# Target and source passes of a graph kernel: bias and one product change engines, edge weights copied earlier

## The chip, the cores and the metric

The kernel runs on one core of one Trainium2 chip. The metric is the device time of one execution in microseconds. Before the change it is 4458.62 us, the median of three runs (4454.08 to 4461.81).

## What is computed

Four graph layers over 100000 nodes of 128 features, 25000 edges sorted by target. Every layer ends in `x = layernorm(x + layer(x))`.

```python
# layer 0: attributes of the edges summed at their target, a small network, residual
agg = segment_sum(e_flat, dst)                      # 160 wide
h = (softplus(agg @ W1.T + b1) - log 2) @ W2.T + b2
x = layernorm(x + (x + h))
# layer 1: weighted neighbours, divided by max(sum of edge weights, 1)
# layer 2: relu(x @ w_s + segment_sum((x @ w_n)[src], dst))
# layer 3: relu(cheb(x, W1, b1)) (256 wide), then cheb(h, W2, b2), three terms each
```

Most nodes are the target of no edge. For them every layer depends on the node's own row alone. Only nodes that are a target get sums from edges.

## The kernel before

An edge pass or a row pass works on quads: 4 tiles of 128 rows, 512 rows in a turn. 25000 edges make 49 quads (`QUADS`), the nodes 196 blocks. The passes run one after the other, with a seam (`enter`, `leave`) at which all five engines wait for each other:

- `tgt0` (the target pass): layer 0 at the targets of the edges, 49 turns, about 310 to 666 us
- `src0` (the source pass): for the sources of the edges, all layers as if no edge came in, stored as state 1, 2, 3 and the hidden state h, 49 turns, about 666 to 1177 us
- `nodes`: the same for all nodes, 196 turns, up to about 2580 us
- `L1`, `L2`, `T1`, `T2`, `LH`, `LU`: the layers with their edge sums, 49 turns each

Every engine runs its own list of instructions in order, written out by hand for turn g, with stages of older quads (`g.less(k)`, in the code g1 to g5) in the same turn. Semaphores (`signal`, `transfer`) order the engines. `s.wait(engine, pass, g, back=k)` waits until the signal of turn g - k is given. Most tiles have two buffers (`g.b`), `rows` has four (`g.r`, `RING`).

**Target pass.** SP loads 512 rows of edge attributes into `rows` three turns ahead (L437). POOL copies the edge weights beside them as column 160 (`put_weights`, L551) and gathers the targets' rows of x by four indirect DMAs (`gather`, L540), which wait for DVE's L880 of two turns before, since `xin` has two buffers. In a turn POOL gathers first and copies for turn g + 2 behind that. PE's turn (L1402) is: transposes for quad g + 1 (L1316, L1318; they wait for `attr_in` and `ew_put`), first product of quad g (L1329, L1330), the sums of weights turned into a column by 1x1 products (L1334), second product of quad g - 1 (L1387). DVE's turn is L849, two scans (L810), L864, then for quad g - 2 L877, L880, the moments (L818, L822), and the marks for the next quad (L791). ACT computes the softplus of quad g - 1, the norm of g - 3 and the root of g - 2.

**Source pass.** POOL's turn: y0 of quad g + 1 (L575), gathers for g + 3 (L540). DVE's turn: statistics of y0 (L926, L931), L959, L962, L969, four L976 (y1), four L982 (x1), L990 (u2), its statistics, L1011, L1014, L1018 (reciprocal `rs1`), and four L1022: the second state x2 of quad g - 1 into `x3b`, a row scaled by `rs1`. ACT's turn: copies of the transposed y0 and y1, L1211 (relu of the 256-wide h of quad g - 4, from PSUM into `hb`), two roots (L1081), the copy yTc, the squares (L1223), x3 (L1234). PE's turn: three groups of transposes (L1298), L1441, L1447, and last h of quad g - 3: for each of four tiles L1466 (one row of ones times the bias row, 256 wide) and L1467 added onto it; before these it waits for `h_kept` of the turn before. SP stores x1, x2, x3 and h in this order (L472).

## Time and profile before

| | |
|---|---|
| median of 3 runs | 4458.62 us |
| the profiled execution | 4466.06 us, of which its span is 4464.0 us |
| PE busy | 3560.5 us (80%) |
| DVE busy | 3173.4 us (71%) |
| ACT busy | 2444.6 us (55%) |
| POOL busy | 3007.1 us (67%) |
| mean granted TensorE clock | 0.889 |

The page gives averages over passes with different limits. A pass is therefore read by a view of its own stretch: the busy time in it, the waits in it, and one turn in order of time. "Idle before" in square brackets is how long the engine stood before an instruction, and what ended that; "issue" is an end that the profile doesn't see. Instructions of one line that follow each other are merged ("x4"). "PEld" (weight loads) is left out below. PE shows a float32 product as two passes.

### The profile page before, as it was taken

The page shows a single profiled execution, that of the slowest core. Times are in us where ns is not written, and L with a number is a line of the kernel's source. Part 1 is how long each engine was busy: PE and PEld are TensorE (multiplying, and loading weights), DVE is VectorE, ACT ScalarE, POOL GpSimd, SP SyncE. Part 2 cuts the span into 40 slices and gives each one's busy share as a digit, 9 for nine tenths or more (in the row PEclk, how much of TensorE's full clock was granted, in tenths as well). Part 3 has the DMA queues.
Part 4 walks back from the last instruction along what each step waited for, and adds up shares of the span by engine and source line. Part 5 has one row for each costly group of instructions (what it writes and reads, how often), then busy time and mean ns, then how long its engine had stood idle before and what let it go on. Part 6 is the DMA issues. An engine that isn't in the chain of part 4 may idle for free. (4 is left out here: it accounts for less than half of the span.)

```text
span 4464.0 us, 77093 instructions
## 1 busy us (share of the span) xinstructions
PE 3560.5 (80%) x21778; PEld 2728.0 (61%) x21778; DVE 3173.4 (71%) x13414; ACT 2444.6 (55%) x7163; POOL 3007.1 (67%) x3450
## 2 busy tenths in 40 slices
PE   6868887999899999999999956566898989931111
PEld 3336655766588888888888746565455768831111
DVE  8988876677588888888888868788222446655555
ACT  0006665666588888888888856311565764421111
POOL 0006656555388888888888767576775757767777
PEclk9989997888899999999999978888999999965555
DMA  0015643444222222222222235454676987843332
GB/s 19 1 45 155 166 133 127 164 166 167 100 77 77 77 76 77 76 76 76 77 77 77 68 123 156 127 157 143 221 247 217 310 288 247 260 140 93 98 94 77
DMA packets 307439, 575.11 MB, mean 129 GB/s; under 512 B 65310, under 2 KB 93783, under 8 KB 307018
## 3 DMA queue, kind: packets, MB, share of 16 engines
q1 hardware_dynamic: 234890, 442.75, 29.4%
q0 software_dynamic: 72128, 127.43, 10.9%
q8 instruction: 180, 2.95, 0.3%
q14 instruction: 241, 1.97, 0.1%
HBM read 300.83 MB, written 270.68 MB: 128 GB/s over the span
## 5 line engine op out<-in xcount | busy, mean ns | idle before, releaser
L1316 PE MATMUL ps<-ident,rows 128*128 128x128 f32 x1372 | 280.9, 310 | 605.2 <-ACT rows L1093 498.3
L540 POOL DMA_INDIRECT rows<-state,rows_of_src x588 | 557.4, 948 | 252.6 <-issue 171.7
L1093 ACT ACTIVATE rows<-rows,lap_w 128x128 f32<-128x128 f32 (+1 forms) x784 | 270.7, 419 | 607.3 <-DMA rows<-lap,rows_of_lap 480.0
L1316 PEld LDWEIGHTS ps<-ident,rows 128*128 128x128 f32 x1372 | 191.4, 159 | 672.7 <-ACT rows L1093 453.6
L810 DVE TENSOR_TENSOR_SCAN x<-same,x,ps 128x512 f32<-128x512 uint8 x336 | 429.0, 1277 | 236.5 <-PE ps L1316 204.6
L1076 ACT ACTIVATE yTa<-ps 128x512 f32<-128x512 f32 x392 | 233.5, 596 | 607.8 <-PE ps L1298 607.6
L540 POOL DMA_INDIRECT rows<-lap,rows_of_lap x392 | 390.5, 996 | 168.5 <-issue 117.1
L618 POOL DMA_INDIRECT lk<-node_table,look_idx x392 | 384.6, 981 | 92.1 <-issue 83.6
L575 POOL TENSOR_TENSOR y<-xin,c0h 128x512 f32<-128x512 f32 x245 | 310.8, 1269 | 200.0 <-DVE outb L982 142.6
L926 DVE BATCH_NORM_STATS2 bn<-y 128x6 f32<-128x128 f32 x1764 | 378.6, 276 | 42.8 <-POOL y L575 42.7
L1454 PE MATMUL ps<-V,hT 128*128 128x128 f32 x3136 | 402.0, 281 | 5.5 <-ACT hT L1206 5.5
L593 POOL TENSOR_SCALAR x<-u,negm,rs 128x128 f32<-128x128 f32 x784 | 342.2, 446 | 74.6 <-DVE rs L959 74.0
L1454 PEld LDWEIGHTS ps<-V,hT 128*128 128x128 f32 x3136 | 364.8, 191 | 43.1 <-ACT hT L1206 43.1
L1461 PE MATMUL ps<-yTc,G 128*128 128x512 f32 x784 | 369.0, 593 | 1.9 <-ACT yTc L1076 1.9
L1298 PEld LDWEIGHTS ps<-ident,y 128*128 128x128 f32 x1960 | 251.3, 151 | 149.6 <-issue 133.9
L1241 ACT ACTIVATE outb<-y,off,rs 128x128 f32<-128x128 f32 x784 | 322.6, 491 | 0.4 <-DVE off L954 0.4
L1298 PE MATMUL ps<-ident,y 128*128 128x128 f32 x1960 | 280.5, 290 | 36.5 <-POOL y L575 33.5
L1223 ACT ACTIVATE unused<-y 128x128 bf16<-128x128 f32 x980 | 290.3, 313 | 0.0
L1441 PE MATMUL ps<-A,yTa 128*128 128x128 f32 x1960 | 288.6, 292 | 1.8 <-ACT yTa L1076 1.7
L540 POOL DMA_INDIRECT xin<-in_x_dram,dst_g x196 | 197.4, 1007 | 136.1 <-DVE y L880 90.7
L976 DVE SCALAR_TENSOR_TENSOR y<-ps,rs,b1c 128x128 f32<-128x128 f32 x980 | 276.2, 345 | 17.2 <-PE ps L1441 6.7
L1081 ACT ACTIVATE sd<-mv,consts 128x4 f32<-128x4 f32 x588 | 174.2, 296 | 192.1 <-DVE mv L822 139.4
(253 smaller groups left out, 9601.1 us busy)
## 6 DMA issues: line engine op xcount, KB each, us to landing
state_h<-hb SPq DMA_DIRECT2D x98, 512.0 KB, 3.9
xin<-in_x_dram SPq DMA_DIRECT2D x196, 256.0 KB, 2.8
out_dram<-outb SPq DMA_DIRECT2D x196, 256.0 KB, 2.1
xe<-state SPq DMA_DIRECT2D x147, 256.0 KB
state<-outb SPq DMA_DIRECT2D x98, 256.0 KB, 2.1
state<-oe SPq DMA_DIRECT2D x98, 256.0 KB, 2.1
h_pre<-hb SPq DMA_DIRECT2D x49, 512.0 KB, 3.1
rows<-in_edge_attr_10x_dram SPq DMA_DIRECT2D x48, 320.0 KB, 3.2
```

The lines of the kernel that those rows point to most:

```text
L540: gp.indirect_dma_start(out=dest[:, at, k, 0:width], out_offset=None, in_=table_, in_offset=bass.IndirectOffsetOnAxis(ap=index[:, c:c + 1] ...
L575: gp.tensor_tensor(y0[:, g.b], xin[:, g.b], all4(c0h[:, :]), ALU.add).then_inc(y0_made.sem, 1)
L593: i = gp.tensor_scalar(x3[:, g2.b, k, :], u2[:, g2.b, k, :], negm[:, g2.b, k:k + 1], rs[:, 2, g2.b, k:k + 1], ALU.add, ALU.mult)
L618: gp.indirect_dma_start(out=lk[:, g.b, 2 * j:2 * j + 2], out_offset=None, in_=node_table, in_offset=bass.IndirectOffsetOnAxis(ap=look_idx[ ...
L810: v.tensor_tensor_scan(t[0:np_, g.b].rearrange("p k d -> p (k d)"), same[0:np_, 512 * g.c:512 * g.c + 512], ps[0:np_, bk + g.b, :], t[0:np ...
L926: i = v.bn_stats(bn[:, n, k, :], y[:, k, :])
L1223: i = a.activation(unused[:, k, :], y1[:, g1.b, k, :], ACT.Square, accum_out=ssum[:, g1.b, k:k + 1])
L1241: i = a.activation(outb[:, g5.b, k, :], y3[:, g5.b, k, :], ACT.Identity, bias=off3[:, g5.b, k:k + 1], scale=rs[:, 3, g5.b, k:k + 1])
L1298: i = t.transpose(bank(bk)[:, k, :], source[:, k, :], ident[:, :])
L1316: i = t.transpose(bank(g.b)[:, k, :], rows[:, g.r, k, 0:P], ident[:, :])
L1454: i = t.matmul(bank(7)[:, k, :], hT[:, j, k, :], V02[:, j, :], start=j == 0, stop=j == 1)
L1461: i = t.matmul(ps[:, 5 + j, :], G02[:, j * P:(j + 1) * P], yTc[:].rearrange("p k d -> p (k d)"), start=True, stop=True)
```

## The change

In the target pass `put_weights` moves in front of the turn's gathers and to turn g + 3, with three copies ahead of the loop, and the four 1x1 products of L1334 become transposes.

In the source pass PE no longer adds the bias: its products start at L1467. DVE adds it, at the end of its turn, from PSUM into `hb` (signal `h_biased`). ACT's relu then runs on `hb` in place, behind x3. The second state is shared: DVE makes tiles 0 to 2 (signal `x2_most`) and POOL tile 3 (signal `x2_made`), in POOL's turn behind the gathers; SP waits for both, and DVE's next write of y1 in that buffer waits for POOL's. PE's last step waits for `h_biased` instead of `h_kept`.

```diff
--- before.py
+++ after.py
@@ -239,7 +239,8 @@
         u2_made, bn2, mv2, tv2, rs2 = (signal(n, "src0 nodes") for n in ("u2_made", "bn2", "mv2", "tv2", "rs2"))
         y3_made, bn3, mv3, rs3, off3_made, looked_up = (
             signal(n, "nodes") for n in ("y3_made", "bn3", "mv3", "rs3", "off3_made", "looked_up"))
-        x1_made, rs1, x2_made, off2 = (signal(n, "src0") for n in ("x1_made", "rs1", "x2_made", "off2"))
+        x1_made, rs1, x2_made, x2_most, h_biased, off2 = (
+            signal(n, "src0") for n in ("x1_made", "rs1", "x2_made", "x2_most", "h_biased", "off2"))
 
         same_made, ew_put, ws_turned, ws_taken, ws_max = (
             signal(n, "tgt0") for n in ("same_made", "ew_put", "ws_turned", "ws_taken", "ws_max"))
@@ -469,6 +470,8 @@
                                                 (x3_made, g.less(2), state3, x3, x3_st), (h_kept, g.less(4), state_h, hb, h_st)):
                     if g_.inside(QUADS):
                         signal_.wait(sp, "src0", g_)
+                        if signal_ is x2_made:
+                            x2_most.wait(sp, "src0", g_)
                         sp.dma_start(quad_of(t, g_, 1), buf[:, g_.b]).then_inc(tr.of(g_), 16)
 
             enter(sp, "src0")
@@ -556,11 +559,11 @@
                     last = g.less(-3)
                     summed.wait(pool, "tgt0", last, back=RING)
                     gp.memset(rows[:, last.r, 3, 0:ATTR], 0.0).then_inc(zeroed, 1)
+                put_weights(g.less(-3))
                 gather("tgt0", g, x, dst_g, xin, g.b, P, x_gathered, [(step, 2)])
-                put_weights(g.less(-2))
-
-            put_weights(Turn(0))
-            put_weights(Turn(1))
+
+            for c in range(3):
+                put_weights(Turn(c))
 
             run_turns(QUADS, 0, tgt0_turn)
             leave(pool)
@@ -576,7 +579,7 @@
 
             def row_pass(p, n, meanwhile):
                 def turn(g):
-                    next_, g2, g3 = g.less(-1), g.less(2), g.less(3)
+                    next_, g1, g2, g3 = g.less(-1), g.less(1), g.less(2), g.less(3)
                     if next_.inside(n):
                         make_y0(p, next_)
                     if p == "nodes" and g3.inside(n):
@@ -584,6 +587,11 @@
                         y3_made.wait(pool, p, g3, back=2)
                         gp.tensor_tensor(x3b[:, g3.b], x3[:, g3.b], all4(gb2_row[:, :]), ALU.add).then_inc(x3b_made.sem, 1)
                     meanwhile(g)
+                    if p == "src0" and g1.inside(n):
+                        rs1.wait(pool, p, g1)
+                        more_st.wait(pool, p, g1, back=2)
+                        gp.tensor_scalar(x3b[:, g1.b, 3, :], y1[:, g1.b, 3, :], rs[:, 1, g1.b, 3:4], None, ALU.mult)\
+                            .then_inc(x2_made.sem, 1)
                     if p == "nodes" and g2.inside(n):
 
                         x3_turned.wait(pool, p, g2, back=2)
@@ -972,6 +980,8 @@
                         p1_made.wait(dve, p, g)
                         y1_turned.wait(dve, p, g, back=2)
                         squared.wait(dve, p, g, back=2)
+                        if not nodes:
+                            x2_made.wait(dve, p, g, back=2)
                         for k in range(4):
                             i = v.scalar_tensor_tensor(y1[:, g.b, k, :], bank(3)[:, k, :], dev(0, g.b, k), b1c[:, :],
                                                        ALU.mult, ALU.add)
@@ -1018,9 +1028,13 @@
                             v.reciprocal(rs[:, 1, g1.b, :], sd[:, 1, g1.b, :]).then_inc(rs1.sem, 1)
                             rs1.wait(dve, p, g1)
                             more_st.wait(dve, p, g1, back=2)
-                            for k in range(4):
+                            for k in range(3):
                                 i = v.tensor_scalar(x3b[:, g1.b, k, :], y1[:, g1.b, k, :], dev(1, g1.b, k), None, ALU.mult)
-                            i.then_inc(x2_made.sem, 1)
+                            i.then_inc(x2_most.sem, 1)
+                    if i3 and not nodes:
+                        h_made.wait(dve, p, g3)
+                        h_st.wait(dve, p, g3, back=2)
+                        v.tensor_tensor(hb[:, g3.b], wide(5), all4(gb1_row[:, :]), ALU.add).then_inc(h_biased.sem, 1)
 
                 enter(dve, p)
                 run_turns(n, 5, turn)
@@ -1205,10 +1219,6 @@
                         for j in range(2):
                             a.activation(hT[:, j], bank(5 + j), ACT.Relu, bias=gb1_col[:, j:j + 1])\
                                 .then_inc(hidden.sem, 1)
-                    if g4.inside(n) and not nodes:
-                        h_made.wait(act, p, g4)
-                        h_st.wait(act, p, g4, back=2)
-                        a.activation(hb[:, g4.b], wide(5), ACT.Relu).then_inc(h_kept.sem, 1)
                     if g2.inside(n):
                         root(p, g2, sd2, tv2, sd[:, 2, g2.b, :], tmpv[:, g2.b, :], EPS2)
                     if g.inside(n):
@@ -1234,6 +1244,9 @@
                             i = a.activation(x3[:, g2.b, k, :], u2[:, g2.b, k, :], ACT.Identity, bias=off3[:, g2.b, k:k + 1],
                                              scale=rs[:, 2, g2.b, k:k + 1])
                         i.then_inc(x3_made.sem, 1)
+                    if g4.inside(n) and not nodes:
+                        h_biased.wait(act, p, g4)
+                        a.activation(hb[:, g4.b], hb[:, g4.b], ACT.Relu).then_inc(h_kept.sem, 1)
                     if nodes and g5.inside(n):
                         off3_made.wait(act, p, g5)
                         out_st.wait(act, p, g5, back=2)
@@ -1331,7 +1344,7 @@
                                  start=False, stop=True).then_inc(first_product.sem, 1)
                         ws_taken.wait(pe, p, g, back=1)
                         for k in range(4):
-                            i = t.matmul(ps[:, 4, k:k + 1], agg_b[32:33, g.b, k, :], ones[32:33, 0:1], start=True, stop=True)
+                            i = t.transpose(ps[:, 4, k:k + 1], agg_b[32:33, g.b, k, :], ident[32:33, 32:33])
                         i.then_inc(ws_turned.sem, 1)
                     if p == "L1":
                         own, near = SELF[g.b], NEIGH[g.b]
@@ -1461,10 +1474,9 @@
                                 i = t.matmul(ps[:, 5 + j, :], G02[:, j * P:(j + 1) * P], yTc[:].rearrange("p k d -> p (k d)"),
                                              start=True, stop=True)
                         else:
-                            h_kept.wait(pe, p, g3, back=1)
+                            h_biased.wait(pe, p, g3, back=1)
                             for k in range(4):
-                                t.matmul(wide(5)[:, k, :], ones[0:1, :], gb1_row[0:1, :], start=True, stop=False)
-                                i = t.matmul(wide(5)[:, k, :], yTc[:, k, :], G02[:, :], start=False, stop=True)
+                                i = t.matmul(wide(5)[:, k, :], yTc[:, k, :], G02[:, :], start=True, stop=True)
                         i.then_inc(h_made.sem, 1)
 
                 enter(pe, p)
```

## Rows read from the trace of the kernel before

**Rows 1.** Stretches: busy us by engine in five columns, granted clock, DMA share, GB/s.

```profile
330.00:650.00 320.00, 281.38 (x1685) 201.49 (x1684) 271.20 (x743) 209.16 (x464) 194.75 (x230) 0.99 0.56 156
...
720.00:1140.00 420.00, 415.75 (x1956) 292.32 (x1955) 301.02 (x1552) 263.04 (x851) 213.50 (x207) 0.87 0.46 164
...
2620.00:2900.00 280.00, 181.18 (x1234) 168.92 (x1232) 224.13 (x767) 151.53 (x459) 189.61 (x201) 0.85 0.47 144
```

**Rows 2.** Waits, 330 to 650 us: total, times, longest.

```profile
POOL xin L540 <- DVE y L880: 88.8, 46, 16.5
```

**Rows 3.** Timeline of one target turn: start us, duration us, engine, line.

```profile
500.06 0.30 PE L1316 MATMUL ps<-ident,rows 128*128 128x128 f32 x1 [0.56 <-issue]
...
500.88 0.69 DVE L880 TENSOR_TENSOR y<-y,xin 128x512 f32<-128x512 f32 x1
...
501.85 0.97 POOL L540 DMA_INDIRECT xin<-in_x_dram,dst_g  x1 [1.89 <-DVE y L880]
...
502.81 0.66 DVE L791 TENSOR_TENSOR same<-dst_in 128x512 uint8<-128x512 int32 x1
...
504.05 0.16 DVE L849 TENSOR_SCALAR tmpv<-ps 128x4 f32<-128x4 f32 x1 [0.58 <-PE ps L1334]
...
506.79 0.21 POOL L551 COPY rows<-ew_col 128x4 f32<-128x4 f32 x1
...
507.09 0.30 PE L1316 MATMUL ps<-ident,rows 128*128 128x128 f32 x1 [1.10 <-issue]
...
507.38 0.69 DVE L880 TENSOR_TENSOR y<-y,xin 128x512 f32<-128x512 f32 x1
```

**Rows 4.** Timeline, DVE: L877 in turns 0 and 46 of the target pass.

```profile
337.66 0.69 DVE L877 SCALAR_TENSOR_TENSOR y<-ps,b2h 128x512 f32<-128x512 f32 x1 [0.99 <-PE ps L1387]
...
649.22 0.65 DVE L877 SCALAR_TENSOR_TENSOR y<-ps,b2h 128x512 f32<-128x512 f32 x1
```

**Rows 5.** Timeline of one source turn, around PE's last step.

```profile
902.41 0.18 DVE L959 RECIPROCAL rs<-sd 128x4 f32<-128x4 f32 x1 [2.80 <-ACT sd L1081]
...
903.11 0.69 PE L1466 MATMUL ps<-gb_row,ones 1*128 1x256 f32 x2
...
907.37 0.88 DVE L1022 TENSOR_SCALAR x3b<-y,rs 128x128 f32<-128x128 f32 x4
...
908.16 0.87 DVE L926 BATCH_NORM_STATS2 bn<-y 128x6 f32<-128x128 f32 x4
...
908.24 1.91 PE L1298 MATMUL ps<-ident,y 128*128 128x128 f32 x8
...
909.06 0.38 DVE L931 BATCH_NORM_AGGREGATE mv<-bn 128x2 f32<-128x6 f32 x4
```

**Rows 6.** Timeline, DVE: L976 in turns 4 and 48 of the source pass.

```profile
720.95 1.13 DVE L976 SCALAR_TENSOR_TENSOR y<-ps,rs,b1c 128x128 f32<-128x128 f32 x4
...
1137.92 1.13 DVE L976 SCALAR_TENSOR_TENSOR y<-ps,rs,b1c 128x128 f32<-128x128 f32 x4
```

**Rows 7.** Opening of the source pass (timeline), and L1022's durations in ns (min/median/max).

```profile
703.26 2.38 DVE L1022 TENSOR_SCALAR x3b<-y,rs 128x128 f32<-128x128 f32 x4
...
703.65 1.27 POOL L575 TENSOR_TENSOR y<-xin,c0h 128x512 f32<-128x512 f32 x1
...
L1022 DVE TENSOR_SCALAR x3b<-y,rs x196: 273/282/1755, 695.5 to 1148.9; 128x128 f32<-128x128 f32 x196
```

**Rows 8.** Durations of nearest operations (ns min/median/max; last row: busy, mean ns).

```profile
L996 DVE TENSOR_TENSOR y<-ps,x3b x196: 679/681/692, 1207.4 to 2570.6; 128x512 f32<-128x512 f32 x196
...
L860 DVE TENSOR_TENSOR hT<-ps,y x25: 1224/1225/1225, 3419.0 to 3662.6; 128x1024 f32<-128x1024 f32 x25
...
L593 POOL TENSOR_SCALAR x<-u,negm,rs x784: 441/444/459, 1193.0 to 2559.1; 128x128 f32<-128x128 f32 x196
...
L1081 ACT ACTIVATE sd<-mv,consts 128x4 f32<-128x4 f32 x588 | 174.2, 296 | 192.1 <-DVE mv L822 139.4
```

**Rows 9.** Timeline, PE: a 256-wide pair at the end of the source pass.

```profile
1155.86 1.22 PE L1467 MATMUL ps<-G,yTc 128*128 128x256 f32 x2
```


## What I expect

> **What bounds the kernel now.** I read the busy time by stretch first [rows 1]. The change touches two passes. In the target pass (330 to 650 us) no engine is full: PE is busy 281 of 320 us, DVE 271, POOL 195. In the source pass (720 to 1140 us) PE is full, 416 of 420 us. So the first is held by a loop of waits, the second by PE's own work.
>
> Target pass: the waits say who stands still [rows 2]. POOL waits 88.8 us for DVE's L880 in 46 turns. A wait alone is no cause, so I follow one turn in time [rows 3]. L880 ends at 501.57 (500.88 + 0.69); POOL's first gather starts at 501.85; four gathers and then the copy of the edge weights (L551) at 506.79, over at 507.0; PE's transposes restart at 507.09. The reader should see that PE starts within 0.1 us of the copy's end although the profile calls the wait "issue": the copy is the last of PE's inputs. From there PE needs 500.06 to 504.05 = 3.99 us to give DVE its weight column, and DVE needs 504.05 to 507.38, plus 0.69, = 4.02 us to the end of the next L880. The loop spans two turns: 0.28 + 5.24 (501.85 to 507.09) + 3.99 + 4.02 = 13.53, or 6.77 us a turn. The measured one is (649.22 - 337.66)/46 = 6.773 us [rows 4]. They agree, so the loop is the bound.
>
> Source pass: in one turn PE runs its last step, eight pairs of 256-wide matmuls, from 903.11 to 908.24 = 5.13 us, and goes straight into the next turn [rows 5]. DVE stands 2.80 us before L959, because ACT's relu (L1211) waits behind PE and stands before the root that L959 needs. The turn is (1137.92 - 720.95)/44 = 9.48 us [rows 6].
>
> **Target pass, the change.** The copy moves before the gathers and one turn further ahead. It waits for the transposes four turns before the row that it fills, which PE finished over a turn earlier, so it runs while POOL stands before its gathers (1.9 us a turn, 88.8/46 [rows 2]) and leaves the loop. Behind it in POOL's queue are only the gathers of the same turn. The four one-column products become transposes, one pass of four instead of two; PE was not the bound, so that is costed at nothing as long as DVE is late. What is late next is DVE's own chain: 504.05 to 507.38 = 3.33, then 500.88 to 502.81 = 1.93, then L791's 0.66 = 5.92 us [rows 3]. PE has 281/(320/6.77) = 5.95 us of work [rows 1] before the four passes leave; it fits, barely. POOL has 5.24 us. So 6.77 becomes 5.92: 0.85 a turn, 46 turns, 39 us. One doubt: the copy (about 0.2 us) now falls at L880, which reads two SBUF tiles; if they exclude each other it costs up to 0.2 us x 46 = 9 us, or nothing if the copy yields. I take 36 us, range 28 to 41.
>
> **Source pass, what leaves.** Four of eight pairs on PE: half of 5.13, so PE's turn falls to about 6.9 us at today's mean clock. ACT's relu moves behind the work that DVE waits for, so the 2.80 us goes. PE is no longer the bound; DVE is next. Its chain from starts [rows 5]: L959 to L1022 902.41 to 907.37 = 4.96; L1022's four products 0.79 (to 908.16); L926 to L931 0.90; L931 to L959 about 0.3 (four aggregates, 0.38 long, overlapped). Sum 6.95.
>
> **Source pass, what comes.** One product leaves DVE: -0.20. The bias comes, one 128x1024 addition from PSUM plus SBUF; the T2 pass has that shape at 1.22 us (L860) and it overlaps its neighbour a little [rows 8]: +1.2. With the relu gone DVE still waits for one short ACT root between L931 and L969: the root takes 0.296 us [rows 8], and L959 and L962 run meanwhile; I estimate +0.14, between 0 and 0.3. That is 8.09 us without interference. ACT has 263/(420/9.48) = 5.9 us of work a turn [rows 1] and PE 6.9, both below. The product on POOL costs 0.444 us there [rows 8]; POOL's turn is 0.28 (its reaction to L880, [rows 3]) + 0.44 + 1.27 (L575, [rows 7]) + 4.94 (four gathers, 501.85 to 506.79) and another 0.28 = 7.2 us, below 8.1. But it is in front of the next L575 and, through that, the next gathers: both slip from behind L982 to behind L1018. L575's result is first used by L926 a whole turn after the one at 908.16; the slip, L982 to L1018, is well under half a turn and is covered. SP's store of the second state waits a little longer, and three stores queue behind it; hb has two buffers, so its store has about a turn to land: no cost. PE waits for DVE's bias of the turn before instead of ACT's relu: it is done before PE comes to that step.
>
> **The unknown cost is DVE against POOL.** When the pass starts, L1022 began at 703.26 and four products took 2.38 us instead of 0.87, while POOL's L575 ran from 703.65 to 704.92 [rows 7]. The longest product took 1755 ns against a median of 282, so it ended (705.01) just after POOL's instruction had. So a SBUF-to-SBUF product of DVE stands still during a POOL instruction on SBUF. L996, from PSUM, ran 196 times beside busy POOL in 679 to 692 ns [rows 8]; the new bias is of that kind and safe. The new POOL product, however, is released by the very reciprocal that releases DVE's three products, and L575 follows it at once. Bounds: nothing, if DVE gets its three in first; +0.25 a turn, if POOL's product stops one of them and DVE gets in before L575; +1.5, if DVE stands until L575 is over (0.28 + 0.44 + 1.27 + 0.1 = 2.1 us after the reciprocal, against 0.7 unhindered, and one or two products after that). I take +0.25: 8.35 us a turn, nearest to the row in which exactly one instruction of POOL was sat out.
>
> The Trainium skill, SBUF — State Buffer, section Who interferes with whom, says that VectorE and GpSimd share one port pair as an exclusive lock, that the one that issues first keeps it for its whole instruction, and that the other fully blocks. By that rule, the trace agrees: the one long L1022 took 1755 ns against 282. The rule speaks against this change, since both products are released together; by it alone the block would last 0.44 us, near my value, if the lock is free between two POOL instructions.
>
> Sum: 44 turns x (9.48 - 8.35) = 50 us. At both ends of the pass the pairs run at the low clock level, 1.22 us each [rows 9]: one step of four fewer at the start, two at the end, 4.9 us each, less the bias and relu that now follow the last one and what other engines hold back: 11 us. Source pass 61, target pass 36, together 97. The profiled execution took 4466.1 us (span 4464.0), so 4369; it lies 7.4 above the median 4458.6, so **4362 us**.
>
> **Rivals.** (a) DVE first, no block: 8.09 a turn, 44 x 1.39 + 11 + 36 = 108, **4351 us**. For it: DVE reacts faster than POOL. Chance 0.17. (b) The lock passes straight from POOL's product to L575: 9.6 a turn, 44 x (-0.12) + 11 + 36 = 42, **4417 us**. For it: POOL's instructions stand in its queue with satisfied waits, and in [rows 7] POOL kept DVE out before its own record began. Against: no row shows DVE skipped twice. Chance 0.27. (c) The copy was not alone last in the target pass, some other input of PE arrives with it and the turn stays near 6.7: 61 only, **4398 us**. Against: the loop adds up to 6.77 with it. Chance 0.07. (d) In the source pass something of the chain ACT, PE, DVE holds the turn near 8.9: 25 + 11 + 36 = 72, **4387 us**. Chance 0.06. (e) Slower: the clock. PE's granted clock was 0.87 in the source pass although PE was full, 0.99 in the target pass at 88% busy, and 0.85 in the L1 pass at 65% [rows 1]. PE falls to some 70% busy. If it stayed at the low level (1.2 GHz) all through, PE's turn would be (9.48 - 5.13) x 0.87/0.5 = 7.6, plus 4 x 1.22 = 4.9, = 12.5 us: 44 x 3.0 = 133 lost, 36 + 11 won, **4545 us**. It binds once over a third of a turn is at the low level, and costs time overall from about three quarters. Against: the L1 pass is no busier and has 0.85. Chance 0.03.
>
> **How the numbers follow.** My forecast has 0.40. The range takes in (a) and (b) with the doubt on the copy: 4340 to 4428, leaving out (e) and tails. A measurement of this kernel tells 0.2% (9 us) from no change. Faster 0.94, same 0.03 (a poor (b) with a poor target pass), slower 0.03.
>
> **What the profile after would show.** L877's starts 5.9 us apart, POOL's copy in its idle time, PE's wait before L1316 gone or ended by DVE. In the source pass L976 8.3 apart, DVE over 90% busy, no 2.80 us wait before L959. The group of L1022's three products tells the cases apart: (a) 0.67 us, forecast about 0.9, (b) over 2. L540 and L575 must follow POOL's product. The prediction is wrong if DVE's three products and L575 overlap otherwise than said, if the turn is set by PE at a granted clock under 0.7, or if L877's period stays over 6.3.

## The result and the profile after

| | before | after |
|---|---|---|
| median of four runs | 4457.76 us | 4344.89 us (4341.65 to 4350.78) |
| the profiled execution | 4466.06 us, span 4464.0 | 4350.78 us, span 4348.7 |
| mean granted TensorE clock | 0.889 | 0.902 |

The ratio is 0.9748 [0.9731, 0.9765]: 113 us faster. The forecast was 4362, so 17 us too slow, inside its range.

Lines have moved: L877 is now L885, L880 is L888, L810 is L818, L540 is L543, L551 is L554, L575 is L578, L926 is L934, L931 is L939, L959 is L967, L976 is L986, L1018 is L1028, L1022 is L1032, L1081 is L1095, L1467 is L1479. New are POOL's product at L593 and DVE's bias at L1037.

Stretches of the changed kernel, columns as in [rows 1]: the target pass, the source pass, the L1 pass.

```profile
330.00:610.00 280.00, 253.49 (x1496) 168.42 (x1494) 268.97 (x739) 204.10 (x459) 198.87 (x227) 0.99 0.60 178
680.00:1060.00 380.00, 254.78 (x1633) 212.17 (x1631) 353.47 (x1575) 270.73 (x864) 248.52 (x254) 0.99 0.54 193
2500.00:2790.00 290.00, 184.93 (x1284) 172.18 (x1285) 235.72 (x809) 156.15 (x470) 199.27 (x212) 0.87 0.48 147
```

DVE is now the fullest engine in both passes: 269 of 280 us and 353 of 380. PE fell to 67% of the source pass, and its granted clock rose from 0.87 [rows 1] to 0.99.

The target pass: the wait of POOL and of PE, over 330 to 600 us (total, times, longest), and then DVE's L885 of turns 0 and 45 with one turn between them in order of time.

```profile
POOL xin L543 <- DVE y L888: 39.6, 42, 12.9
PE ps L1342 <- DVE x3b L818: 26.5, 44, 0.7
```

```profile
336.86 0.69 DVE L885 SCALAR_TENSOR_TENSOR y<-ps,b2h 128x512 f32<-128x512 f32 x1 [0.65 <-PE ps L1400]
...
502.36 0.27 PE L1329 MATMUL ps<-ident,rows 128*128 128x128 f32 x1
...
503.98 1.12 PE L1342 MATMUL ps<-x,W1Ta 128*128 128x512 f32 x2 [0.58 <-DVE x3b L818]
...
504.60 0.78 DVE L888 TENSOR_TENSOR y<-y,xin 128x512 f32<-128x512 f32 x1
...
505.25 0.21 POOL L554 COPY rows<-ew_col 128x4 f32<-128x4 f32 x1
...
605.32 0.65 DVE L885 SCALAR_TENSOR_TENSOR y<-ps,b2h 128x512 f32<-128x512 f32 x1
```

L888 and the copy L554 over the whole pass (ns, minimum, median, maximum):

```profile
L888 DVE TENSOR_TENSOR y<-y,xin x49: 691/718/778, 337.6 to 624.1; 128x512 f32<-128x512 f32 x49
L554 POOL COPY rows<-ew_col x49: 189/199/767, 310.5 to 594.2; 128x4 f32<-128x4 f32 x49
```

The period is (605.32 - 336.86)/45 = 5.97 us, against 6.77 [rows 4]. PE's wait before the transposes is gone. What it waits for now is DVE's scan. POOL's copy (505.25) no longer stands behind the gathers. The turn shown has the longest L888 of all, 0.78 us instead of 0.69 [rows 3]; the median is 0.72, and where no copy runs beside it L888 stays at 0.69. In about a quarter of the turns it is the copy that gets longer, up to 0.77 us instead of 0.20, and L888 stays at 0.69 to 0.70.

One source turn of the changed kernel, against [rows 5]:

```profile
860.38 0.17 DVE L1028 RECIPROCAL rs<-sd 128x4 f32<-128x4 f32 x1
860.59 0.84 DVE L1032 TENSOR_SCALAR x3b<-y,rs 128x128 f32<-128x128 f32 x3
860.65 0.69 POOL L593 TENSOR_SCALAR x3b<-y,rs 128x128 f32<-128x128 f32 x1 [1.08 <-DVE rs L1028]
...
861.30 1.21 DVE L1037 TENSOR_TENSOR hb<-ps,gb_row 128x1024 f32<-128x1024 f32 x1
861.33 1.26 POOL L578 TENSOR_TENSOR y<-xin,c0h 128x512 f32<-128x512 f32 x1
...
862.44 0.85 DVE L934 BATCH_NORM_STATS2 bn<-y 128x6 f32<-128x128 f32 x4
...
863.33 0.38 DVE L939 BATCH_NORM_AGGREGATE mv<-bn 128x2 f32<-128x6 f32 x4
863.62 0.14 DVE L967 RECIPROCAL rs<-sd 128x4 f32<-128x4 f32 x1
863.74 0.30 ACT L1095 ACTIVATE sd<-mv,consts 128x4 f32<-128x4 f32 x1 [2.25 <-DVE mv L939]
...
864.57 1.99 PE L1479 MATMUL ps<-G,yTc 128*128 128x256 f32 x8 [1.65 <-ACT yTc L1090]
```

DVE goes from one instruction to the next without a wait. ACT waits for it (2.25 us), and PE for ACT (1.65 us). The turn, from L986 of turn 4 to that of turn 48, against [rows 6]:

```profile
676.68 1.12 DVE L986 SCALAR_TENSOR_TENSOR y<-ps,rs,b1c 128x128 f32<-128x128 f32 x4
...
1035.71 1.12 DVE L986 SCALAR_TENSOR_TENSOR y<-ps,rs,b1c 128x128 f32<-128x128 f32 x4
```

That is 359.03/44 = 8.16 us instead of 9.48. The durations of the two halves of the shared product (ns, minimum, median, maximum):

```profile
L1032 DVE TENSOR_SCALAR x3b<-y,rs x147: 281/326/404, 657.6 to 1045.2; 128x128 f32<-128x128 f32 x147
L593 POOL TENSOR_SCALAR x3b<-y,rs x49: 623/695/722, 659.4 to 1044.8; 128x128 f32<-128x128 f32 x49
```

By their starts, DVE's second product follows the first after 0.20 us, as in the kernel before, and the third follows the second after 0.32 us instead of 0.20; so the bias behind them starts 0.12 us later, in nearly every turn. The durations overlap and say less. POOL's 695 ns can't be set against the 444 of [rows 8], a median over products of the node pass that follow each other four at a time: in the bias-first run below this product takes 603 ns with no product of DVE beside it, and 602 with no instruction of DVE beside it at all (1062.89 us). So POOL's loses 0.09 us.

**Where the 115 us of span went.** The source pass's first y0 starts 38.0 us earlier (640.55 against 678.51): the target pass. The node pass's first y0 starts 117.9 us earlier (1061.17 against 1179.07), so the source pass gave 79.9: 44 turns 57.9, its opening (from the first y0 to L986 of turn 4) 6.3, its end 15.7. The later passes took back 2.6.

### The profile page after: what moved, and what is told of

It reads as the page before. It is cut to its first block and busy times, and to the rows that moved or that the text cites. A ratio compares the mean times of both kernels' runs of the same rounds, so it can differ in the third digit from the quotient of the medians.

```text
span 4348.7 us, 76062 instructions
## 1 busy us (share of the span) xinstructions
PE 3337.6 (77%) x21190; PEld 2595.4 (60%) x21190; DVE 3221.5 (74%) x13414; ACT 2442.3 (56%) x7163; POOL 3051.8 (70%) x3499
## 5 line engine op out<-in xcount | busy, mean ns | idle before, releaser
L543 POOL DMA_INDIRECT rows<-state,rows_of_src x588 | 557.0, 947 | 249.2 <-issue 173.2
L818 DVE TENSOR_TENSOR_SCAN x<-same,x,ps 128x512 f32<-128x512 uint8 x336 | 428.9, 1276 | 237.5 <-PE ps L1329 204.0
L543 POOL DMA_INDIRECT rows<-lap,rows_of_lap x392 | 391.7, 999 | 167.3 <-issue 117.7
L1467 PE MATMUL ps<-V,hT 128*128 128x128 f32 x3136 | 402.7, 282 | 5.7 <-ACT hT L1220 5.7
L934 DVE BATCH_NORM_STATS2 bn<-y 128x6 f32<-128x128 f32 x1764 | 378.2, 275 | 23.4 <-POOL y L578 23.3
L1467 PEld LDWEIGHTS ps<-V,hT 128*128 128x128 f32 x3136 | 365.4, 192 | 43.2 <-ACT hT L1220 43.2
L1095 ACT ACTIVATE sd<-mv,consts 128x4 f32<-128x4 f32 x588 | 174.1, 296 | 276.5 <-DVE mv L939 152.9
L578 POOL TENSOR_TENSOR y<-xin,c0h 128x512 f32<-128x512 f32 x245 | 311.1, 1270 | 15.9 <-DMA xin<-in_x_dram 15.9
L1311 PEld LDWEIGHTS ps<-ident,y 128*128 128x128 f32 x1960 | 232.8, 143 | 146.2 <-issue 130.6
L1311 PE MATMUL ps<-ident,y 128*128 128x128 f32 x1960 | 259.9, 276 | 37.1 <-POOL y L578 34.7
L986 DVE SCALAR_TENSOR_TENSOR y<-ps,rs,b1c 128x128 f32<-128x128 f32 x980 | 276.2, 344 | 14.0 <-PE ps L1454 3.9
L1454 PEld LDWEIGHTS ps<-A,yTa 128*128 128x128 f32 x1960 | 242.1, 194 | 56.7 <-ACT yTa L1090 46.7
```

The costliest lines, as they stand in the source:

```text
L543: gp.indirect_dma_start(out=dest[:, at, k, 0:width], out_offset=None, in_=table_, in_offset=bass.IndirectOffsetOnAxis(ap=index[:, c:c + 1] ...
L578: gp.tensor_tensor(y0[:, g.b], xin[:, g.b], all4(c0h[:, :]), ALU.add).then_inc(y0_made.sem, 1)
L818: v.tensor_tensor_scan(t[0:np_, g.b].rearrange("p k d -> p (k d)"), same[0:np_, 512 * g.c:512 * g.c + 512], ps[0:np_, bk + g.b, :], t[0:np ...
L934: i = v.bn_stats(bn[:, n, k, :], y[:, k, :])
L1311: i = t.transpose(bank(bk)[:, k, :], source[:, k, :], ident[:, :])
L1454: i = t.matmul(bank(3)[:, k, :], yTa[:, k, :], A1[:, :], start=True, stop=True)
```

## The experiments

My theory: in the target pass the copy is the last link of the loop; in the source pass DVE sets the turn, and POOL's product costs it little because it doesn't fall beside POOL's long instruction. The rivals: PE's fewer passes, not the copy, shorten the target turn; POOL's product is worth nothing or harms; the relu's new place did it; and PE lost its time not to the amount of bias work but to how that work was cut. Runs of one group shared a chip with runs of the kernel before. A source turn is the mean over 44 turns, read as above.

### First group: the two halves, and the two edits of the target pass

The kernel before took 4460.24 us here.

**The target edits alone**: the changed kernel, with the source pass of before.

```diff
-                            h_biased.wait(pe, p, g3, back=1)
+                            h_kept.wait(pe, p, g3, back=1)
                             for k in range(4):
-                                i = t.matmul(wide(5)[:, k, :], yTc[:, k, :], G02[:, :], start=True, stop=True)
+                                t.matmul(wide(5)[:, k, :], ones[0:1, :], gb1_row[0:1, :], start=True, stop=False)
+                                i = t.matmul(wide(5)[:, k, :], yTc[:, k, :], G02[:, :], start=False, stop=True)
```

> The kernel before with the target pass's two edits alone. My theory: the two passes are independent, so this keeps the whole target gain, about 38 us (period of L877's line 6.77 to 5.97 us), and the source pass stays at 9.48 us a turn: about 4420 us, ratio 0.9915. Rival: part of the later passes' gain comes from shifted phases, then the two single-pass kernels don't add up to the 113 us of both.

Measured: 4417.7 us, ratio 0.9902 [0.9882, 0.9921], 42.5 us less. The target turn is 5.97, the source turn stays near 9.5.

**The source edits alone**: the changed kernel, with the target pass of before.

```diff
-                put_weights(g.less(-3))
                 gather("tgt0", g, x, dst_g, xin, g.b, P, x_gathered, [(step, 2)])
+                put_weights(g.less(-2))
...
-                            i = t.transpose(ps[:, 4, k:k + 1], agg_b[32:33, g.b, k, :], ident[32:33, 32:33])
+                            i = t.matmul(ps[:, 4, k:k + 1], agg_b[32:33, g.b, k, :], ones[32:33, 0:1], start=True, stop=True)
```

> The kernel before with the source pass's edits alone. My theory: the source pass gains 80 us, of which 58 in 44 steady turns (9.48 to 8.16 us) and 22 at its opening and its end; the target pass stays at 6.77 us: about 4378 us, ratio 0.982. Rival as for the target edits: the sum of both differs from 113 us by over 5.

Measured: 4386.0 us, 0.9833 [0.9816, 0.9851], 74.2 less. The source turn is 8.17, the target turn alternates 6.45 and 7.08, mean 6.77. The halves add up to 116.7 against 113 for both, inside the intervals: no sign that the two parts share a bound.

**The copy alone**: the kernel before, the copy moved, the 1x1 products kept.

```diff
+                put_weights(g.less(-3))
                 gather("tgt0", g, x, dst_g, xin, g.b, P, x_gathered, [(step, 2)])
-                put_weights(g.less(-2))
```

> The kernel before with only the copy of the edge weights moved; the four one-column products stay products. Theory A (the copy was the last link of a two-turn loop, 13.5 us): the period falls to about 6.0 us, set by PE's 5.95 us of work and DVE's 5.9; gain 35 us or more of the 38. Rival B (the shorter weight column on PE was the gain): the period stays above 6.5 us, gain under 12 us.

Measured: 4421.95 us, 0.9916 [0.9898, 0.9934], 38.3 less. Its timeline, two following L877:

```profile
500.50 0.65 DVE L877 SCALAR_TENSOR_TENSOR y<-ps,b2h 128x512 f32<-128x512 f32 x1
...
506.46 0.65 DVE L877 SCALAR_TENSOR_TENSOR y<-ps,b2h 128x512 f32<-128x512 f32 x1
```

5.96 us, and 6.01 as the mean over 46 turns: the copy alone gives nearly the whole gain in the turn. It was the last link of the loop.

**The transposes alone**: the kernel before, the 1x1 products turned into transposes, the copy left behind the gathers.

```diff
-                            i = t.matmul(ps[:, 4, k:k + 1], agg_b[32:33, g.b, k, :], ones[32:33, 0:1], start=True, stop=True)
+                            i = t.transpose(ps[:, 4, k:k + 1], agg_b[32:33, g.b, k, :], ident[32:33, 32:33])
```

> The kernel before with only the four one-column products made transposes. Theory A: the loop of two turns gets shorter by the passes that leave, some 0.5 to 0.6 us, so the period falls from 6.77 to about 6.5: gain 12 us. Rival B: period about 6.0 us, gain 35 us or more.

Measured: 4439.26 us, 0.995 [0.9934, 0.9966], 21.0 less where some 12 were expected. Its timeline:

```profile
490.50 0.65 DVE L877 SCALAR_TENSOR_TENSOR y<-ps,b2h 128x512 f32<-128x512 f32 x1
497.29 0.65 DVE L877 SCALAR_TENSOR_TENSOR y<-ps,b2h 128x512 f32<-128x512 f32 x1
...
503.89 0.20 POOL L551 COPY rows<-ew_col 128x4 f32<-128x4 f32 x1
504.19 0.30 PE L1316 MATMUL ps<-ident,rows 128*128 128x128 f32 x1 [1.49 <-issue]
```

Turns of 6.11 and 6.79 us alternate, mean 6.45. PE still starts right behind the copy. So what leaves PE here shortens its share of the loop across two turns: in the trace of the kernel before the eight passes of the 1x1 products take 1.05 us (502.96 to 504.01), here the four of the transposes take 0.40, and 0.65 us over two turns is the step from 6.77 to 6.45. That is 15 us in 46 turns. The rest is of the size by which unedited turns vary: those of the source pass take 9.36 here, 9.41 and 9.53 in the copy-only and target-only runs, and 0.1 us is 4 us in the pass. With the copy moved that share is no longer in any loop, and the transposes add nothing: costing them at nothing was right beside the copy, not alone.

### Second group: the source pass

The kernel before took 4457.67 us here.

**The bias with full rows.** Does PE lose its time to the amount of work, or to the single row of ones? Kernel before, with 128 rows of 1/128 against the bias row that stands in all 128 partitions: the same sum, the same number of matmuls, one of 128 rows instead of one.

```diff
+            v.tensor_scalar(even[:, :], ones[:, :], 1.0 / P, None, ALU.mult)
...
-                                t.matmul(wide(5)[:, k, :], ones[0:1, :], gb1_row[0:1, :], start=True, stop=False)
+                                t.matmul(wide(5)[:, k, :], even[:, :], gb1_row[:, :], start=True, stop=False)
```

> The kernel before, but the bias product of the source pass is made from 128 rows of 1/128 instead of one row of ones: as many instructions and columns, all partitions in use. Theory A (PE's low clock stretches came with the one-row products): granted clock in the source pass 0.97 or more instead of 0.87, turn about 8.5 us instead of 9.48, gain about 45 us, without any work leaving PE. Rival B (the clock falls for another reason, such as the whole load of the pass): clock and time unchanged.

Measured: 4344.02 us, 0.9748 [0.9731, 0.9764]: 113.7 us less, as much as the whole change, with nothing taken from PE. The expected 45 us missed. Its stretch 720 to 1040 us, and its PE and weight loads in the last step:

```profile
720.00:1040.00 320.00, 307.02 (x1960) 275.41 (x1959) 301.82 (x1559) 263.37 (x847) 212.31 (x207) 1.00 0.62 218
```

```profile
898.12 0.59 PE L1467 MATMUL ps<-gb_row,even 128*128 128x256 f32 x2
...
898.34 0.41 PEld L1468 LDWEIGHTS ps<-G,yTc 128*128 128x128 f32 x2
...
898.55 0.59 PE L1468 MATMUL ps<-G,yTc 128*128 128x256 f32 x2
```

The same step of the kernel before:

```profile
903.73 0.30 PEld L1467 LDWEIGHTS ps<-G,yTc 128*128 128x128 f32 x2 [0.33 <-issue]
```

```profile
903.73 0.70 PE L1467 MATMUL ps<-G,yTc 128*128 128x256 f32 x2
904.36 0.69 PE L1466 MATMUL ps<-gb_row,ones 1*128 1x256 f32 x2
```

Two things changed. The clock went from 0.87 to 1.00. And pairs now follow each other 0.43 us apart instead of 0.63: with equal rows the load of the next pair begins 0.21 us ahead of its product (898.34 against 898.55), while before both begin together (903.73) and PEld had stood for 0.33 us. The turn is 7.17 us. One cause had been expected and two acted; the third group parts them. DVE no longer stands before L959 (here L960) either, although ACT's relu is in its old place and still waits for PE. Over 720 to 1040 us:

```profile
DVE rs L960 <- ACT sd L1082: 4.0, 20, 0.9
```

In the kernel before the same wait comes to 110.5 us over 720 to 1140 us.

**All four products on DVE.** The changed kernel with POOL's product given back.

```diff
-                            for k in range(3):
+                            for k in range(4):
                                 i = v.tensor_scalar(x3b[:, g1.b, k, :], y1[:, g1.b, k, :], dev(1, g1.b, k), None, ALU.mult)
```

> The changed kernel with all four products of the second state back on DVE, the bias still on DVE. Theory A (the product on POOL saves DVE 0.20 us and costs it 0.13 by the shared SBUF access): 0.07 us a turn slower, 8.22 us, some 3 us in all, which can't be told from no change. Rival B (POOL's product is worth its full 0.20): 8.36 us a turn, 9 us slower. Rival C (the product on POOL costs more than it saves): faster than the changed kernel.

Measured: 4354.26 us, 0.9773 [0.9757, 0.979], turn 8.25. In a steady turn POOL's product is worth 0.09 us, some 4 us in 44 turns: the 0.20 that leaves DVE, less the 0.12 that its other three then lose. The medians lie further apart, 9.4 us, and so do the whole source passes, 429.1 against 420.6 us from first y0 to first y0: 3.9 of the 8.5 are in the 44 turns, 1.0 in the opening, 3.6 at the end. So the 9 us of rival B came out in the time, but not by its turn of 8.36; why the end is longer was not tried.

**The bias ahead of the products.** In the changed kernel DVE adds the bias first. Its three products then fall beside POOL's L578.

```diff
+                        v.tensor_tensor(hb[:, g3.b], wide(5), all4(gb1_row[:, :]), ALU.add).then_inc(h_biased.sem, 1)
+                    if i1 and not nodes:
...
+                        for k in range(3):
+                            i = v.tensor_scalar(x3b[:, g1.b, k, :], y1[:, g1.b, k, :], dev(1, g1.b, k), None, ALU.mult)
```

> The changed kernel with DVE's bias ahead of its three products of the second state, so that POOL's product and L578 (0.7 and 1.27 us) are under way when DVE comes to the products 1.2 us later. Theory A (a SBUF-to-SBUF product of DVE stands until the POOL instruction is over): one product of each three lasts about 0.9 us, the three take 1.3 to 1.5 us instead of 0.84, POOL's product takes 0.44 us instead of 0.70 since nothing stands against it, and the turn goes from 8.16 to about 8.7 us: 25 us slower than the changed kernel. Rival B (the two only slow each other a little): under 5 us slower, turn below 8.3.

Measured: 4368.43 us, 0.9807 [0.979, 0.9824], turn 8.66.

```profile
L593 POOL TENSOR_SCALAR x3b<-y,rs x49: 602/603/720, 654.8 to 1062.9; 128x128 f32<-128x128 f32 x49
...
859.55 1.20 DVE L1032 TENSOR_TENSOR hb<-ps,gb_row 128x1024 f32<-128x1024 f32 x1
...
859.73 0.60 POOL L593 TENSOR_SCALAR x3b<-y,rs 128x128 f32<-128x128 f32 x1 [1.20 <-DVE rs L1028]
...
860.32 1.26 POOL L578 TENSOR_TENSOR y<-xin,c0h 128x512 f32<-128x512 f32 x1
...
860.66 1.45 DVE L1037 TENSOR_SCALAR x3b<-y,rs 128x128 f32<-128x128 f32 x3
```

L578 is over at 861.58. DVE's three products start at 860.66 and end at 862.11: 1.45 us instead of 0.84. The first of them lasts 1009 ns, to 861.67, and the other two are through 0.44 us later. So POOL's long instruction does keep a SBUF product of DVE out until it is over. That DVE is also passed over between two instructions of POOL, which rival (b) needed, no run shows. In the changed kernel no product is kept out like that, since DVE's products are through (861.43) about when L578 begins (861.33), and what then runs beside L578 is the bias from PSUM, which took 1.21 us as expected. The order of DVE's last two steps is worth 23.5 us by the medians, and 44 x (8.66 - 8.16) = 22 by the turns. POOL's product takes 0.60 us here, not the 0.44 expected.

**Three products on ACT.** DVE's turn is what counts, and ACT stands 2.25 us in each. ACT makes the three products, one turn later, behind the first of its two roots, where it stood those 2.25 us.

```diff
+                    if g2.inside(n) and not nodes:
+                        rs1.wait(act, p, g2)
+                        more_st.wait(act, p, g2, back=2)
+                        for k in range(3):
+                            i = a.activation(x3b[:, g2.b, k, :], y1[:, g2.b, k, :], ACT.Copy, scale=rs[:, 1, g2.b, k:k + 1])
+                        i.then_inc(x2_most.sem, 1)
```

> The changed kernel with DVE's three products of the second state made by ACT in its wait before the root (2.25 us long in each turn), SP's store one turn later. Theory A (DVE's chain is the bound, every microsecond taken from it is gained): DVE loses 0.72 us, turn 7.44 us, 34 us faster than the changed kernel, about 4311 us. Rival B (ACT and PE's chain takes over): ACT has 5.8 plus 1.3 us of work; if its order with PE holds the turn at 7.9 or above, the gain is under 13 us.

Measured: 4311.05 us, 0.9671 [0.9653, 0.9688], turn 7.40. This beats both the changed kernel and the full-rows one. Its stretch 680 to 1000 us:

```profile
680.00:1000.00 320.00, 241.07 (x1562) 201.60 (x1561) 303.04 (x1381) 291.66 (x951) 239.23 (x252) 1.00 0.61 214
```

DVE and ACT are both nearly full now (303 and 292 of 320).

### Third group: one row, 32 rows, 128 rows

These ran on a chip where the kernel before takes 4737.82 us (4717.31 to 4753.72) and the later passes last longer; they are compared among themselves and by the turn.

**Fewer changes between kinds.** The kernel before, with the one-row products in pairs of tiles.

```diff
+                            for pair in ((0, 2), (1, 3)):
+                                for k in pair:
+                                    t.matmul(wide(5)[:, k, :], ones[0:1, :], gb1_row[0:1, :], start=True, stop=False)
+                                for k in pair:
+                                    i = t.matmul(wide(5)[:, k, :], yTc[:, k, :], G02[:, :], start=False, stop=True)
```

> The kernel before with the same eight pairs in the source pass's last step in another order: two one-row bias products, then the two products of their tiles, twice. Theory A (what makes a 256-wide instruction take 0.63 us instead of 0.43 there is the change between one row and 128 rows, eight changes a turn): four changes are left, 4 x 0.2 = 0.8 us less, turn about 8.6 us, gain 35 us or more. Theory B (one-row products are slow in themselves, in any order): the turn stays above 9.2 us.

Measured: 4690.47 us, 0.9908 [0.9882, 0.9934], turn 8.45. Its stretch, and one step:

```profile
720.00:1040.00 320.00, 311.81 (x1671) 247.41 (x1670) 257.05 (x1327) 223.26 (x718) 195.02 (x190) 0.90 0.53 188
```

```profile
844.68 1.13 PE L1467 MATMUL ps<-gb_row,ones 1*128 1x256 f32 x4 [0.20 <-issue]
845.73 1.13 PE L1469 MATMUL ps<-G,yTc 128*128 128x256 f32 x4
846.79 1.13 PE L1467 MATMUL ps<-gb_row,ones 1*128 1x256 f32 x4
```

Four passes of a kind take 1.06 us, where two times 0.63 = 1.26 were needed: each change between kinds that is left out saves 0.2 us. The clock stays low, 0.90.

**32 rows.** The kernel before, with 32 rows of 1/32.

```diff
+                                t.matmul(wide(5)[:, k, :], even[0:32, :], gb1_row[0:32, :], start=True, stop=False)
```

> The kernel before with the bias product made from 32 rows of 1/32. If only a full 128 rows bring the gain of the 128-row run (turn 9.48 to 7.16 us), the pairs keep their 0.63 us and the turn stays above 9 us; the granted clock may rise a little. If the single row was the odd case, the turn is near 7.2 us.

Measured: 4709.27 us, 0.995 [0.9933, 0.9966], turn (1099.50 - 723.30)/44 = 8.55.

```profile
720.00:1040.00 320.00, 312.01 (x1656) 212.86 (x1655) 252.73 (x1303) 220.63 (x716) 190.12 (x185) 0.99 0.52 183
```

```profile
1005.27 0.69 PE L1467 MATMUL ps<-gb_row,even 32*128 32x256 f32 x2 [0.21 <-issue]
1005.89 0.70 PE L1468 MATMUL ps<-G,yTc 128*128 128x256 f32 x2
```

The clock is 0.99, the pairs are still 0.63 apart. So the two effects part: from 9.48 to about 8.5 us a turn is the clock, from 8.5 to 7.17 the changes between instructions of few rows and of 128. The kernel before shows the first in its own trace. Its turns swing between 8.46 and 10.83 us, and two that follow each other at full clock are as short as those with 32 rows:

```profile
940.97:957.90 16.93, 16.52 (x88) 11.18 (x88) 13.57 (x71) 11.69 (x39) 10.11 (x10) 1.00 0.49 174
```

16.93/2 = 8.47 us. The total fell by 28 us, less than the some 40 that the turns make. There is no profile of the kernel before from this chip, but an estimate from the four of this group puts most of the rest down to it: they spend 3562 to 3566 us behind the source pass and, where the target pass is unedited, 678 to 681 us ahead of it, which of a span of 4735.8 us leaves some 492 for the source pass before, against the 500.6 between its first y0 and that of the node pass in the first trace (678.51 to 1179.07). With 32 rows it took 459.7.

**The relu early.** The changed kernel with ACT's relu ahead of the roots, where it stood before.

```diff
+                    if g4.inside(n) and not nodes:
+                        h_biased.wait(act, p, g4)
+                        a.activation(hb[:, g4.b], hb[:, g4.b], ACT.Relu).then_inc(h_kept.sem, 1)
                     if g2.inside(n):
                         root(p, g2, sd2, tv2, sd[:, 2, g2.b, :], tmpv[:, g2.b, :], EPS2)
```

> The changed kernel with ACT's relu of h back in its old place before the two roots. Theory A (DVE's wait of 2.80 us came from PE, and the relu's place did nothing once PE is free, since ACT waits 2.25 us before the root anyway): turn stays within 0.05 us of 8.16, no change. Rival B (the place mattered): DVE waits before L967 again and the turn is 8.6 us or more, 20 us slower than the changed kernel.

Measured: 4639.69 us, 0.9806 [0.9778, 0.9834], turn 8.20 (8.16 with the relu late, on the other chip). Where the relu stands is worth next to nothing: DVE's 2.80 us before L959 [rows 5] came from PE being late, and go once PE isn't, as the full-rows run has it too.

**Target edits with full rows.** Both cheap repairs: the copy and the transposes, and the 128-row bias on PE, with nothing moved to DVE, ACT or POOL.

```diff
                             for k in range(4):
-                                i = t.matmul(wide(5)[:, k, :], yTc[:, k, :], G02[:, :], start=True, stop=True)
+                                t.matmul(wide(5)[:, k, :], even[0:128, :], gb1_row[0:128, :], start=True, stop=False)
+                                i = t.matmul(wide(5)[:, k, :], yTc[:, k, :], G02[:, :], start=False, stop=True)
```

> The target pass's two edits together with the 128-row bias product on PE, all else in the source pass as before. The two are in different passes, so they add: 38 to 42 us and 113 us less than before, about 4305 us, 40 us faster than the changed kernel. Rival: the DMA load of the shorter passes takes part of it back; then it is above 4320 us.

Measured: 4615.84 us, 0.9745 [0.9718, 0.9772]: 122.0 less than the kernel before, where over 150 were expected, and no better a ratio than full rows alone had on the other chip (0.9748). It is 23.9 less than the relu-early kernel beside it, not the 40 expected of the changed one. A steady target turn is 5.97. Of 44 source turns 17 take about 7.11, 12 up to 7.6, and 15 take 8.2 to 9.7; the mean is 7.73. The clock is 0.99, so it isn't that. The waits of the source pass (680 to 1020 us) show an end outside the five engines:

```profile
DVE y L977 <- remote: 16.4, 12, 2.5
```

With 2.7 us of the kind before L991 that is as much as 19 of the 25 us by which 44 such turns are longer than 44 of 7.17. The same waits stand in the 32-row and the paired run of this chip (9.8 and 5.6 us), whose target pass is unedited, and in no source pass of the other two groups. So the target edits are not what brings them. They would fit transfers that land late on this chip, but no run tests that: full rows alone did not run here, and the cause of the long turns stays open.

## Why the prediction was right, step by step

**Target pass: right.** Forecast 36 us, 28 to 41; measured 38.0. The loop over two turns closed with the copy as its last link, as the copy-only run shows (5.96 us a turn). What came next was DVE's chain, 5.97 against the 5.92 added up. The doubt was in place and smaller than allowed for: L888's median is 0.03 us longer, 1.2 us in 46 turns and half of the 0.05 by which the period is above 5.92, and in a quarter of the turns the copy yields at no cost. Rival (c) is out. The transposes were costed at nothing for the right reason, by the copy-only run.

The Trainium skill, SBUF — State Buffer, section Who interferes with whom, says that a DVE instruction with two SBUF inputs contends with a GpSimd instruction that reads SBUF. By that rule, the trace agrees: a median of 0.72 us against 0.69, and in other turns a copy of up to 0.77 us instead of 0.20.

**Source pass: the bound is right, two sizes are off.** DVE sets the turn, 8.16 us. Its parts, from starts in order: L967 to L1032 5.12 (forecast 4.96 + 0.14), the three products to the bias 0.72 (0.59 + 0.25), the bias 1.14 (1.2), the moments 0.89 (0.90), back to L967 0.29 (0.3).

- The term for DVE against POOL was mis-sized: 0.13 a turn, not 0.25, 44 x 0.12 = 5.3 us of the 7.9 between 50 and 57.9; most of the rest is the bias, 0.06 cheaper a turn between starts. The forecast had POOL's product stop one whole product of DVE, since [rows 7] shows one that sat out a POOL instruction. Here DVE lost 0.12 us at one place, between its second and third product, and POOL's product 0.09 (695 ns against 603), so neither sat out the other's whole work. The outcome lies nearer to rival (a)'s 8.09 than to the 8.35 forecast. Its reason, that DVE comes first, is borne out: 860.59 against 860.65. POOL's product had been priced at 0.44 us and takes 0.60 by itself; POOL still stands 1.08 us before it, so that cost nothing.
- The opening and end were sized at 11 and gave 22.0. This is the larger of the two misses. The forecast had four pairs of 1.22 us leave each of three steps [rows 9]. Near the end of the pass the step now looks like this in the timeline, eight matmul passes in 1.96 us:

```profile
1051.09 1.96 PE L1479 MATMUL ps<-G,yTc 128*128 128x256 f32 x8 [1.77 <-DVE hb L1037]
```

  So the pairs that stayed also came to full clock. Before, the first step of the pass took 9.27 us (from 707.71) and the last two 8.75 and 9.27 (from 1152.94 and 1163.28); now these three take 1.99, 1.96 and 1.96, which is 21 us less. The low level in [rows 9] had been taken as a property of the pass's end. It isn't one: in the full-rows run, with all eight pairs still on PE, the last step's pairs take 0.59 us:

```profile
1053.14 0.59 PE L1468 MATMUL ps<-G,yTc 128*128 128x256 f32 x2
```

All three terms were sized low: the target pass by 2.0 us, the steady turns by 7.9, opening and end by 11.0, together 20.9; the later passes took back 2.6, which leaves the 18.3 between the 4369 forecast for the profiled execution and its 4350.8.

**Rivals (b) and (d).** That POOL's long instruction holds a product of DVE out is true, by the bias-first run: 1.45 us against 0.84, the turn 8.66. But that run brings it about by having DVE come to its products when L578 is under way. That DVE, released together with POOL, is passed over between POOL's product and L578, as (b) says, did not happen in the changed kernel: its products are through at 861.43. Rival (d), a chain of ACT, PE and DVE at 8.9, is out: both ACT and PE wait in each turn.

**Rival (e) pointed the wrong way.** It read the low clock in the source pass as something that less work would make worse. The clock went from 0.87 to 0.99 as PE's busy share fell from 99% to 67%. With 32 rows or 128 instead of one, and PE at 96 to 98%, it is 0.99 and 1.00. In the source pass it went by the rows of the bias product and a little by their order (0.90 in pairs), not by PE's busy share. The forecast did not foresee the rise either: it counted PE's turn at the mean clock of before. What holds it at 0.87 in the L1 pass was not tried.

**"PE is full, by its own work" was half the truth.** PE was busy 416 of 420 us, but 2.3 of the 9.48 us of a turn were low clock and changes of kind, which 128 rows take away without moving any work. The steady turn of the forecast did not need this, since DVE sets it; the opening and the end did, and were missed by it. As a diagnosis it missed that as much as the whole change brought could be had with one edit on PE.

## What to carry to other kernels

When engines wait for each other over two turns, add up the loop and look at the last link into it: here a copy of 0.2 us behind four gathers cost 0.8 us a turn, and nothing else in the pass had to change. Where a bias is added on PE as one row times ones between products of 128 rows, try all 128 rows (ones/128 against a bias that stands in every partition) before moving it to another engine; here that was worth 113.7 us on one chip, and with the target edits 122.0 on another. If work does move to DVE, set DVE's SBUF-to-SBUF steps and POOL's long instructions apart in time, with a step from PSUM beside POOL, and look for an engine with a wait in each turn (ACT's 2.25 us) for what DVE can shed.

## What the runs showed of the hardware

- Two-pass matmuls of 256 columns follow each other 0.43 us apart when both have 128 rows, and 0.63 when one-row or 32-row ones alternate with 128-row ones. The 0.2 us belong to the change of kind (four passes between changes take 1.06). In the alternating case the weight load starts with its matmul, in the equal case 0.21 us ahead; that the late load is what costs the time is an inference from this.
- The Trainium skill, TensorE: Matmul & The Clock Gate, section Step-by-step: what each phase is for, says that weight loads are pulled ahead of running matmuls when the row groups don't conflict or the load goes to the background weight buffer, and that the number of rows doesn't matter to a load's time. The trace agrees on the time (0.29 and 0.30 us for two loads of one row and of 128). It shows the loads ahead among equal rows and not ahead at a change of kind; which of the two conditions fails there no run here shows.
- The granted clock in the middle of the source pass was 0.87 with one-row products, 0.90 with them in pairs, 0.99 with 32 rows, 1.00 with 128, 0.99 without them.
- A product of 128x128 from SBUF to SBUF on POOL took 602 ns by itself, 444 ns as the median in the node pass, where four are issued together, and 695 ns released together with DVE's three. Of these the third started 0.12 us late.
- A SBUF product of DVE that came 0.34 us after a 1.26 us instruction of POOL had begun lasted until that was over, 1009 ns; DVE's bias from PSUM beside the same instruction took 1.21 us, as long as 1.22 for that shape in [rows 8].
